# High and low halves of q and k for both heads at once, placed by DMA, and row maxima laid out by ScalarE and DMA

## What is computed

```python
q = einsum('bse,hde->bhsd', x, Wq) + bq[None, :, None, :]
k = einsum('bse,hde->bhsd', x, Wk) + bk[None, :, None, :]
v = einsum('bse,hde->bhsd', x, Wv) + bv[None, :, None, :]
scores = einsum('bhsd,bhtd->bhst', q, k) / sqrt(dh)
scores = where(causal, -inf, scores)
att = softmax(scores, axis=-1) / sqrt(dh)
z = einsum('bhst,bhtd->bhsd', att, v).reshape(b, s, h * dh)
x = x + z @ proj
```

## Time and profile before

| | us |
|---|---|
| median of 3 runs | 1237.49 (1237.07 to 1238.51) |
| profiled execution | 1247.1 |
| its span | 1245.3 |
| TensorE busy | 1112.4 |
| VectorE busy | 796.8 |
| ScalarE busy | 698.4 |
| GpSimd busy | 539.4 |
| the 16 units of the first attention | from about 45 to 640 |

### The profile page before, as it was taken

One profiled execution on the slowest core, in us unless ns is written; L12 is line 12 of the kernel. 1 busy time (PEld: TensorE's weight loads), 2 busy tenths in 40 slices (PEclk: granted clock), 3 DMA queues, 4 the chain that ended last, 5 costly groups with the idle time before them and its releaser, 6 DMA issues.

```text
span 1245.3 us, 16734 instructions
## 1 busy us (share of the span) xinstructions
PE 1112.4 (89%) x5836; PEld 591.6 (48%) x5836; DVE 796.8 (64%) x1587; ACT 698.4 (56%) x943; POOL 539.4 (43%) x445
## 2 busy tenths in 40 slices
PE   5699999999999999999964779999999949999998
PEld 2345445544454545455423532222322228878876
DVE  5677776877777877777735332223322158999998
ACT  3254554554554544554422049998999837666664
POOL 1265655655655565655640000000000015878876
PEclk9799999999999999999985579999999968999999
DMA  3111111111111111111200000000000000311210
GB/s 103 32 41 24 35 38 26 41 33 31 35 32 33 41 32 26 41 33 26 66 1 1 0 3 11 11 11 8 12 11 10 10 4 3 127 63 66 84 51 34
DMA packets 34888, 40.22 MB, mean 32 GB/s; under 512 B 19380, under 2 KB 22084, under 8 KB 33788
## 3 DMA queue, kind: packets, MB, share of 16 engines
q1 hardware_dynamic: 34812, 39.23, 12.5%
HBM read 19.23 MB, written 1.11 MB: 16 GB/s over the span
## 4 chain that ended last, share of the span: by engine, by line
PE 58%; DVE 27%; issue 9%; ACT 3%; SPq 1%; POOL 1%; DMA 1%; DVEq 0%; ACTq 0%
PE banks L903 9%; PE banks L377 7%; PE banks L891 6%; PE banks L305 5%; PE banks L362 5%; DVE qb L1208 5%; DVE mxa L541 5%; PE banks L322 4%; PE banks L363 4%; PE banks L396 3%; PE banks L343 3%; PE banks L386 2%; DVE kb L526 2%; DVE zz L576 2%; DVE qb L555 2%
## 5 line engine op out<-in xcount | busy, mean ns | idle before, releaser
L655 POOL TENSOR_TENSOR pacc<-pacc,prob 128x1024 f32<-128x1024 f32 (+3 forms) x160 | 274.0, 1712 | 70.9 <-ACT prob L467 61.4
L467 ACT ACTIVATE prob<-banks 128x1024 f32<-128x1024 f32 x192 | 155.7, 811 | 192.2 <-PE banks L363 157.0
L912 ACT ACTIVATE prob<-banks 128x1024 f32<-128x1024 f32 x256 | 238.8, 1094 | 23.7 <-PE banks L891 23.7
L1241 POOL TENSOR_TENSOR ka<-prob,qb 128x512 fp32r<-128x512 f32 x108 | 165.2, 1551 | 60.3 <-ACT qb L1191 33.8
L377 PE MATMUL banks<-prob,v 128*64 128x512 f32 (+3 forms) x768 | 166.2, 511 | 1.6 <-POOL prob L646 1.6
L362 PE MATMUL banks<-qa,ka 128*128 128x512 f32 (+3 forms) x384 | 158.1, 419 | 5.4 <-ACT prob L467 3.9
L903 PE MATMUL banks<-prob,v 128*32 128x512 f32 x1024 | 137.7, 611 | 1.0 <-DVE pacc L920 0.5
L857 POOL TENSOR_TENSOR sq<-sq 64x512 f32<-64x512 f32 x8 | 8.3, 1032 | 292.4 <-DVE sq L853 292.4
L1197 ACT ACTIVATE prob<-banks,w 128x512 f32<-128x512 f32 x144 | 94.5, 686 | 71.3 <-PE banks L1159 71.3
L646 POOL TENSOR_SCALAR_AFFINE_SELECT prob<-prob 128x256 f32<-128x256 f32 x128 | 52.1, 407 | 183.4 <-ACT prob L467 183.4
L363 PE MATMUL banks<-qb,kb 72*128 72x512 f32 (+3 forms) x384 | 130.8, 349 | 0.0
(11 more groups left out here) (193 smaller groups left out, 1671.9 us busy)
## 6 DMA issues: line engine op xcount, KB each, us to landing
qb<-qa SPq DMA_DIRECT2D x64, 128.0 KB, 2.3
ka<-ka SPq DMA_DIRECT2D x64, 128.0 KB, 2.3
prob<-gate_rows SPq DMA_DIRECT2D x8, 1024.0 KB, 4.5
w<-in_experts SPq DMA_DIRECT2D x9, 514.0 KB, 3.6
wqkv<-in_wqkv SPq DMA_DIRECT2D x16, 193.0 KB, 2.4
x<-in_x SPq DMA_DIRECT2D x4, 256.0 KB, 4.1
zz<-pacc SPq DMA_DIRECT2D x64, 16.0 KB
wpr<-pacc SPq DMA_DIRECT2D x64, 16.0 KB
```

The source lines that it names most:

```text
L467: act.activation(pr[:, j % NRING, :, 0:wd], banks[:, 0:2, 0:wd], ACT.Exp, scale=SCALE0).then_inc(s_exp, 1)
L655: pool.tensor_tensor(pacc[:, sbk, :, o:BLK], pacc[:, sbk, :, o:BLK], pr[:, j % NRING, :, 0:wd], ALU.add).then_inc(s_padd, 1)
L912: act.activation(prob[:, n % NP1, :], banks[:, 2 * (n % 3):2 * (n % 3) + 2, :].rearrange("p b c -> p (b c)"), ACT.Exp, scale=2 * SCALE1).t ...
L1241: pool.tensor_tensor(act2[1][:, tb % 2, i, :], hid[:, tb % 2, i, :], act2[0][:, tb % 2, i, :], ALU.subtract).then_inc(s_hlP, 1)
```

## The change

There are two new tiles `ht` and `lt` of 128 x 4 x 512, one block each for i. `hi_act` makes the high half of a block for both heads with one ACTIVATE of 128 x 512 into `ht`; `lo_dve` makes the low half with one instruction into `lt`. SP then places everything: four copies of 64 x 512 of the high half and two of the low half per block, where before there were two copies. The maxima are made from `ht`.

`mrow_dve` and `mD` go. In their place ScalarE negates the 8 x 128 transposed maxima into `mneg` (`mrow_act`), and SP moves for each head 4 x 128 numbers into one row of `qb` (`mrow_sp`), so that L363 multiplies 65 rows. For the scores at j = 0 and j = 4 TensorE waits for all six copies of each block (96) and the two row copies (32).

```diff
+        def mrow_act(act, n, half):
+            act.wait_ge(s_turn, 2 * n + half + 1)
+            if n > 0:
+                act.wait_ge(s_mrd[half], 32 * n)
+            act.activation(mneg[:, half, :], banks[0:2 * NCH, 4 if half == 0 else 7, 0:P], ACT.Copy, scale=-1.0).then_inc(s_mrow, 1)
...
         def lo_dve(dve, n, w, i):
             half, isk = divmod(i, 2)
-            src, c = banks[:, (2, 3, 7, 6)[i], :], slice(half * BLK, (half + 1) * BLK)
             dve.wait_ge(s_hi0, 4 * n + i + 1)
...
+            if n > 0:
+                dve.wait_ge(s_dup[i], 16 * 6 * n)
+            ins = dve.scalar_tensor_tensor(out=lt[:, i, :], in0=banks[:, (2, 3, 7, 6)[i], :], scalar=wqkv[:, w, 3 * D + isk:3 * D + isk + 1],
+                                           in1=ht[:, i, :], op0=ALU.add, op1=ALU.subtract)
...
             elif j == 4:
-                pe.wait_ge(s_mrow, 2 * u + 2)
-                pe.wait_ge(s_lo0, 4 * u + 4)
-                pe.wait_ge(s_dup[2], 16 * 2 * (u + 1))
-                pe.wait_ge(s_dup[3], 16 * 2 * (u + 1))
+                pe.wait_ge(s_mrd[1], 32 * (u + 1))
+                pe.wait_ge(s_dup[2], 16 * 6 * (u + 1))
+                pe.wait_ge(s_dup[3], 16 * 6 * (u + 1))
...
+        def mrow_sp(sp, n, half):
+            sp.wait_ge(s_mrow, 2 * n + half + 1)
+            for h in range(2):
+                sp.dma_start(qb[DH:KB_ROWS, n % 2, h, half * BLK:(half + 1) * BLK].bitcast(F32),
+                             mneg[h * NCH:(h + 1) * NCH, half, :].bitcast(F32)).then_inc(s_mrd[half], 16)
...
                     sp.wait_ge(s_hi0, 4 * n + i + 1)
...
+                    for h in range(2):
+                        hp, ot = slice(h * DH, (h + 1) * DH), slice((1 - h) * DH, (2 - h) * DH)
+                        first = (ka if isk else qa)[hp, w, h, c].bitcast(F32)
+                        second = ka[ot, w, h, c].bitcast(F32) if isk else qb[0:DH, w, h, c].bitcast(F32)
+                        sp.dma_start(first, ht[hp, i, :].bitcast(F32)).then_inc(s_dup[i], 16)
+                        sp.dma_start(second, ht[hp, i, :].bitcast(F32)).then_inc(s_dup[i], 16)
+                    sp.wait_ge(s_lo0, 4 * n + i + 1)
+                    for h in range(2):
+                        hp, ot = slice(h * DH, (h + 1) * DH), slice((1 - h) * DH, (2 - h) * DH)
+                        low = kb[0:DH, w, h, c].bitcast(F32) if isk else qa[ot, w, h, c].bitcast(F32)
+                        sp.dma_start(low, lt[hp, i, :].bitcast(F32)).then_inc(s_dup[i], 16)
+                    if i == 1 and n > 0:
+                        mrow_sp(sp, n - 1, 1)
+                mrow_sp(sp, n, 0)
```

More of the change, by code:

```diff
@@ L26 @@
 MROWS = 2 * (BLK // P)
-KB_ROWS = DH + MROWS
+KB_ROWS = DH + 1
 NRING = 6
@@ L98, in build_kernel @@
         cst = sb("cst", [P, CONSTS])
-        mD = sb("mD", [MROWS, 2, NCH, P])
+        ht = sb("ht", [P, 4, BLK], F32R)
+        lt = sb("lt", [P, 4, BLK], F32R)
+        mneg = sb("mneg", [2 * NCH, 2, P], F32R)
         msk = sb("msk", [P, BLK])
@@ L201, in build_kernel @@
         s_qk, s_hi0, s_lo0, s_vp, s_v = (sem(n) for n in ("qk_projected", "qk_hi_done", "qk_lo_done", "v_projected", "v_stored"))
+        s_mrd = [sem("max_row_first"), sem("max_row_second")]
         s_dup = [sem(f"{n}_copied") for n in ("q_first", "k_first", "q_second", "k_second")]
@@ L321, in max_pe @@
                     hp = slice(h * DH, (h + 1) * DH)
-                    mm = pe.matmul(banks[:, MAX_BANK[r] + h, at:at + width(s, c)], qa[hp, w, h, s * P:(s + 1) * P],
-                                   ka[hp, w, h, c * BLK:c * BLK + width(s, c)], start=True, stop=True)
+                    mm = pe.matmul(banks[:, MAX_BANK[r] + h, at:at + width(s, c)], ht[hp, 2 * (s // NCH), s % NCH * P:(s % NCH + 1) * P],
+                                   ht[hp, 2 * c + 1, 0:width(s, c)], start=True, stop=True)
             mm.then_inc(s_kp, 1)
@@ L348, in scores_pe @@
             if j == 0:
[L349 to L352, removed]
+                pe.wait_ge(s_mrd[0], 32 * (u + 1))
+                pe.wait_ge(s_dup[0], 16 * 6 * (u + 1))
+                pe.wait_ge(s_dup[1], 16 * 6 * (u + 1))
             elif j == 4:
-                pe.wait_ge(s_mrow, 2 * u + 2)
-                pe.wait_ge(s_lo0, 4 * u + 4)
-                pe.wait_ge(s_dup[2], 16 * 2 * (u + 1))
-                pe.wait_ge(s_dup[3], 16 * 2 * (u + 1))
+                pe.wait_ge(s_mrd[1], 32 * (u + 1))
+                pe.wait_ge(s_dup[2], 16 * 6 * (u + 1))
+                pe.wait_ge(s_dup[3], 16 * 6 * (u + 1))
             if not (first and j == 0):
@@ L471, in hi_act @@
             act.wait_ge(s_qk, 4 * n + i + 1)
[L472 to L475, removed]
+            if n > 0:
+                act.wait_ge(s_dup[i], 16 * 6 * n)
+            ins = act.activation(ht[:, i, :], banks[:, (2, 3, 7, 6)[i], :], ACT.Identity, bias=wqkv[:, w, 3 * D + isk:3 * D + isk + 1])
             ins.then_inc(s_hi0, 1)
+        def mrow_act(act, n, half):
[3 more added lines that the diff above has]
+            act.activation(mneg[:, half, :], banks[0:2 * NCH, 4 if half == 0 else 7, 0:P], ACT.Copy, scale=-1.0).then_inc(s_mrow, 1)
         def v_act(act, n, w, k):
@@ L492, in attn0_act @@
                 hi_act(act, 0, 0, i)
+            mrow_act(act, 0, 0)
             v_act(act, 0, 0, 0)
@@ L504, in unit0_act @@
                     hi_act(act, n, x_, 0)
-                elif j == 2 and not last:
-                    hi_act(act, n, x_, 1)
+                elif j == 2:
+                    mrow_act(act, u, 1)
+                    if not last:
+                        hi_act(act, n, x_, 1)
                 elif j == 3 and not first:
@@ L514, in unit0_act @@
                     hi_act(act, n, x_, 3)
+                elif j == 10 and not last:
+                    mrow_act(act, n, 0)
                 elif j == 11 and not last:
@@ L549, in max_dve @@
             ins.then_inc(s_mx, 1)
[L551 to L557, removed]
         def newton_dve(dve, u, sbk):
@@ L588, in attn0_dve @@
                 max_dve(dve, 0, r, True)
-            mrow_dve(dve, 0, 0, 0)
             for r in range(3, 7):
@@ L608, in unit0_dve @@
                 elif j == 2:
-                    mrow_dve(dve, u, w, 1)
                     if not last:
@@ L632, in unit0_dve @@
                 elif j == 10 and not last:
-                    mrow_dve(dve, n, x_, 0)
                     max_dve(dve, n, 4, False)
@@ L674, in dups_sp @@
                     sp.dma_start(wqkv[:, w, :], a["wqkv"][(n + 2) % PAIRS]).then_inc(s_wq[w], 16)
+            mrow_sp(sp, 2 * PAIRS - 1, 1)
         def units0(e, unit):
@@ L1297, in _ @@
             sp.dma_start(pick[:, :, :], a["pick"]).then_inc(s_wp, 16)
-            sp.dma_start(mD[:, :, :, :].rearrange("r h s c -> r (h s c)"), a["mD"]).then_inc(s_maskd, 16)
             dups_sp(sp)
@@ L1379, in _ @@
             dve.wait_ge(s_cbe, 5)
-            dve.wait_ge(s_maskd, 16)
             attn0_dve(dve)
```

## The result

The changed kernel takes 1357.06 us in the median of four runs (1349.64 to 1365.41), the kernel before 1238.0; the ratio is 1.0955 with a 95% interval of 1.092 to 1.099. The direction was forecast, the size was not: 1303 was predicted, between 1256 and 1345. The profiled execution took 1360.2 us with a span of 1358.4, 113.1 us more than the span before.

The account below looks back on a forecast made before the run. TensorE, busy 89%, was taken as the main bound, VectorE at the unit's end. Per unit + 4.9 + 1.7 - 1.4 - 0.6 = + 4.6 us, fifteen units + 69, less 3 at the start: + 66, forecast 1303 us, range 1256 to 1345.

Parts of the forecast that it names:

- the two places: Where TensorE waits in a first-attention unit: at its end for VectorE's maxima, and mid-unit around second-half scores and out projection.
- Term 2: Mid-unit, before the j=4 scores: the second row queues on SP behind twelve copies, costing 4.9 us a unit after slack.
- Term 3: TensorE's clock: low after the new mid-unit wait, costing 1.7 us a unit; the shorter end wait gives back 0.6.
- Term 1: Unit's end: VectorE loses one low-half instruction and the maxima layout ahead of the next maximum, gaining 1.4 us a unit.
- Term 4: Start before the first unit: fewer half-making and layout instructions on the chain, gaining 3 us.
- The dear end: Upper end of the forecast for the whole kernel: + 108 us, 1345, with the longest wait and dearest low clock.
- the clock stays: Rival: the mid-unit wait comes but TensorE stays at 2.4 GHz; + 41 us, 1278; chance 0.19.
- Crowded copies: Rival: twelve back-to-back copies run at 1 us each, the second row 10.8 us late; near 1390 us; chance 0.09.
- In time: Rival: SP's issues and the row's landing cost TensorE nothing at j=4; 33 us less, 1204; chance 0.04.

Follow-up runs that it names:

- e3: The changed kernel plus 22 matmuls with unused results ahead of TensorE's wait for the second half's row, in units 0 to 14; 1300.39 us, ratio to before 1.0487.
- e7: The changed kernel with only the first half's row copies moved ahead of the last low half's two copies on SP; 1342.1 us, ratio to before 1.0802.
- e6: The changed kernel with both rows earlier on SP, the second half's behind six copies of the next pair, not twelve; 1264.47 us, ratio to before 1.014.
- e1: The changed kernel with the two row copies issued by ScalarE right behind the ACTIVATE that makes the row, not by SP; 1207.31 us, ratio to before 0.974.
- e2: The changed kernel with row copies earlier on SP: second half's behind four copies, first half's ahead of the last low half's two; 1203.8 us, ratio to before 0.9732.
- e5: The kernel before, its halves and copies kept, with only the maxima negated by ScalarE and laid out by SP's row copies; 1273.8 us, ratio to before 1.0253.

## Why the prediction was right in kind and wrong in size

**The bound and the two places** were read rightly. Nothing happened elsewhere: the stretch from j = 6 to r = 3 moved by 0.09 us.

**Term 2, the wait in the middle**, was in its range: + 5.2 us predicted (3.9 to 6.1), + 6.04 measured. Two of its parts were off and partly cancelled. The pace was taken as 0.57, a mean between a first and a second copy of a pair; but the short interval is only that after a wait of SP, every further issue comes 0.64 us after the last, the end of the range. The landing of a row of 2 KB takes 1.65 us, not the 2.2 of the nearest row. For quiet units that gives 13 x 0.64 + 1.65 = 9.97 us, against 10.03 measured. The mean is 10.66, because in eight of the fourteen units one interval on this path is 1.0 to 2.2 us in place of 0.64, which no row ahead of the prediction showed. That twelve copies in a row run at about the pace of the issues was read rightly: the engines were 0.92 busy.

**Term 3, the clock**, is the step that failed. Its direction held in all fifteen units. Its price was put at 1.7 us, half of a stretch of 3.4 us at half speed, with all of that as the upper end; with the slack of 0.23 us the stretch from j = 4 to j = 6 should have grown by 1.5 us. It grew by 3.14, and e3 shows that without the low clock it would have shrunk by 0.5, so the clock cost 3.6. The reason given for the half, that TensorE waits for the exponentials in part of that time, did not hold: it was busy for 6.38 of the 6.4 us from 240.0 to 246.4, all at the low clock. The other error was to take the length of the low stretch from the only case in the trace, a wait of 1.5 us with 3.5 us at 0.52 behind it. After 6.3 us without work, 6.4 us and more were worked at 0.50, and the record is low for 10.2 to 13.7 us a unit, in part while TensorE still waits. The case at hand was four times the wait on record, and the upper end of 3.4 us was drawn from that one case; 3.6 lies just over it. The page TensorE: Matmul & The Clock Gate of the Trainium skill (HAM oscillation — how this bites in real kernels), cited in the prediction, tells of a kernel that starts every piece cold after its DMA wait. The trace agrees in kind: the granted clock over the stretch from j = 4 to j = 6 was 0.50 to 0.58 in all fifteen units.

**Term 1, the relief**, was 2.0 us a unit with its share of the clock, and 1.53 was measured. The reading was sound: in quiet units the first row came 0.4 us too late (5.70 with the row ahead, e7, 6.10 without), inside the 0.2 to 0.7 predicted. What was missing is the long issue again, which lifts five of fourteen units to 7.2 to 7.5. With the row out of the way the relief is 8.12 - 5.70 = 2.4 us, a little more than the 1.55 + 0.6 costed for it without a wait.

**Term 4 and unit 0.** The start gained 4.9 us, not 3. Unit 0 lost 11.4, not 4.6: its records show the low clock for 19.7 us, against 2.3 in the kernel before, and the forecast had no term for that.

In sum the forecast of + 66 misses 47 us: per unit 1.67 in the stretch of the clock, 0.84 in the wait, 0.47 in the relief and 0.09 elsewhere, 3.07 times 14 makes 43; unit 0 adds 7, and the start and the end take off 4, which leaves 1 to rounding. That is in spans. Between 1303 and 1357 lie 54 us; the other 7 come from the step from the profiled execution to the median, for which 9.6 us were taken off and which is 3.2 us after the change. The dear end of 1345 was missed by 12 us: these 7, and 5 for unit 0 and some 0.3 us a unit, less the start and the end.

**The rivals.** That the clock stays was refuted: it fell in every unit. Crowded copies: the time came near to that case, but not by its mechanism; the pace was 0.64 us and not 1, the same as behind a single pair of copies, e6 shows it in doses, and e1 and e2 carry all copies at 1204 to 1207 us. With the engines 0.92 busy there was little room left before that case would have begun. In time: it did not happen, yet its number, 1204 us, is what e2 measured, since that order does bring the row nearly in time; that the numbers are equal to the microsecond is chance.

## What to carry over

A DMA of 2 KB costs its landing plus the issues that stand ahead of it on its queue, and here that was 0.64 us for each; before a small result is sent by DMA, count what is queued before it and put it first, which here was worth 11%. A wait on TensorE must be priced with the work that follows it at the low clock: 6.0 us of wait cost 3.6 more, and the step from a mean wait of 0.3 us (e2) to one of 1.8 (e6) cost 3.9 us a unit, wait and clock together. The idea of the change was sound: with the rows early it beats the kernel before by 2.7%.

## What the runs showed of the hardware

- SP starts copies of 64 x 512 float32 without a wait between them 0.64 us apart, and the sixteen DMA engines are then 0.92 busy at 204 GB/s. In the first attention of the change 13 issues took 1.4 to 2.2 us. Four of them are the 105th, 221st, 337th and 451st DMA of SP in the change as well as in e2, at quite different times (144.7 and 128.3 us for the first), but in e3, where SP's order is that of the change, none of the nine issues over 1.1 us in the first attention is among these four, so the place in the order alone does not decide. What causes them was not tried and stays open.
- From the issue of the second row copy to the release of TensorE it took 1.65 us, with twelve copies of 128 KB just ahead of it in the queue as with four. Where ScalarE issued the pair (e1) it took 2.4 us.
- The low clock came in all units with waits of 5.5 to 7.3 us (the change), in ten of fourteen after 1.6 to 2.7 us (e6), in six of fourteen after 2.4 us (e5), and in none of fourteen after 0.3 to 0.7 us (e2). Between e5 and e6 it does not go with the length of the wait alone; what else decides stays open.
